# Reordering the sync engine's load queue in the cross-attention of a fused decoder layer

## What is computed

```python
q = (Q @ Wq.T).reshape(b, s, H, DK).transpose(0, 2, 1, 3)      # Q = norm(x), H = 16 heads of DK = 16
k = (K @ Wk.T).reshape(b, -1, H, DK).transpose(0, 2, 1, 3)     # K = V = ctx, 120 places a row
v = (V @ Wv.T).reshape(b, -1, H, DK).transpose(0, 2, 1, 3)
score = jnp.einsum('bhqd,bhkd->bhqk', q, k) / jnp.sqrt(jnp.float32(DK))
score = jnp.where(mask == 0, jnp.float32(1e-09), score)
out = jnp.einsum('bhqk,bhkd->bhqd', jax.nn.softmax(score, axis=-1), v)
return out.transpose(0, 2, 1, 3).reshape(b, s, d) @ Wo.T
```

## Time and profile before

| | us |
|---|---|
| median of 3 runs (1132.88 to 1135.84) | 1135.7 |
| the profiled execution | 1124.39 |
| its span, first to last instruction | 1122.6 |
| self-attention, to the barrier | 0 to 437 |
| cross-attention | 437 to 713 |
| experts | 713 to 1123 |

### The profile page before, as it was taken

The page is one execution under the profiler, slowest core; times in us unless marked ns, Lnnn a source line. Parts: engine busy times, 40 slices in busy tenths (PEclk is TensorE's granted clock), DMA queues, the critical chain, the costliest instruction groups (busy, mean ns, idle before and its releaser), DMA issues.

```text
span 1122.6 us, 28508 instructions
## 1 busy us (share of the span) xinstructions
PE 1061.1 (95%) x11049; PEld 913.5 (81%) x11049; DVE 668.2 (60%) x1317; ACT 646.5 (58%) x872; POOL 554.2 (49%) x678
## 2 busy tenths in 40 slices
PE   7799999999999988999998999999999999999995
PEld 6678777777777766777776777899999999999995
DVE  4488888888888878788886888423424222222221
ACT  2466666566666665777775777544454444444441
POOL 5534455453545233433654666567754444444442
PEclk9999999999999999999998999999999999999998
DMA  8674644637355432665665657675432323322322
GB/s 216 161 185 105 167 123 111 179 89 179 106 129 152 112 98 73 172 187 159 136 148 147 145 148 231 215 152 57 45 53 47 53 51 50 48 48 48 48 43 24
DMA packets 174562, 130.22 MB, mean 116 GB/s; under 512 B 60810, under 2 KB 162927, under 8 KB 174432
## 3 DMA queue, kind: packets, MB, share of 16 engines
q1 hardware_dynamic: 155280, 106.79, 36.6%
q0 software_dynamic: 15840, 18.77, 11.6%
q10 hardware_dynamic: 3312, 2.85, 0.9%
HBM read 88.29 MB, written 40.08 MB: 114 GB/s over the span
## 4 chain that ended last, share of the span: by engine, by line
PE 50%; DMA 5%; DVE 1%; ACT 1%; issue 1%; SPq 1%; POOL 0%; POOLq 0%; ACTq 0%
PE ps_scores L1987 22%; PE ps_out L2005 11%; PE ps_turn L1850 4%; PE ps_misc L1882 2%; DMA weights<-q_scr 2%; PE ps_out L1862 2%; PE ps_scores L1837 2%; PE ps_misc L1803 2%; DMA q_scr<-qp 1%; PE ps_turn L1966 1%; PE ps_misc L1870 1%; PE ps_scores L1830 1%; PE ps_misc L1876 1%; SPq L1499 1%; ACT weights L2178 1%
## 5 line engine op out<-in xcount | busy, mean ns | idle before, releaser
L1987 PEld LDWEIGHTS ps_scores<-xgT,weights 128*128 128x128 f32 x2272 | 264.1, 192 | 3.3
L1987 PE MATMUL ps_scores<-xgT,weights 128*128 128x128 f32 x2272 | 265.7, 275 | 0.0
L2476 DVE TENSOR_TENSOR gate<-ps_scores,silu 128x512 f32<-128x512 f32 x71 | 49.1, 692 | 241.3 <-ACT silu L2218 241.2
L956 ACT ACTIVATE weights<-ps_scores 128x1024 f32<-128x1024 f32 x128 | 127.1, 1023 | 78.2 <-PE ps_scores L631 63.7
L2218 ACT ACTIVATE silu<-ps_scores 128x512 f32<-128x512 f32 x71 | 42.4, 597 | 206.2 <-PE ps_scores L1987 206.1
L2005 PE MATMUL ps_out<-w2s,gate 128*128 x560 | 132.6, 380 | 0.8 <-DVE y L2482 0.8
L2211 ACT COPY weights<-weights 128x2048 f32 x68 | 129.9, 1911 | 0.0
L2005 PEld LDWEIGHTS ps_out<-w2s,gate 128*128 128x128 f32 x560 | 101.0, 190 | 11.9 <-issue 1.2
L1130 DVE TENSOR_REDUCE sa_rowmax<-ps_turn 128x8 bf16<-128x1024 f32 x64 | 77.8, 1216 | 34.4 <-PE ps_turn L608 34.3
L961 ACT CAST weights<-ps_scores 8x1024 bf16<-8x1024 f32 x64 | 64.3, 1004 | 54.1 <-PE ps_scores L622 54.1
L1673 POOL DMA_INDIRECT table<-entry,slot_i x64 | 64.9, 1014 | 43.6 <-PE ps_out L1862 19.9
(11 more groups left out here) (325 smaller groups left out, 2104.6 us busy)
## 6 DMA issues: line engine op xcount, KB each, us to landing
weights<-w_scr SPq DMA_DIRECT2D x60, 256.0 KB, 4.2
weights<-q_scr SPq DMA_DIRECT2D x96, 128.0 KB
ks<-w_scr SPq DMA_DIRECT2D x24, 256.0 KB, 3.8
weights<-k_scr SPq DMA_DIRECT2D x48, 120.0 KB, 3.8
w_scr<-wp SPq DMA_DIRECT2D x7, 768.0 KB, 3.9
q_scr<-qp SPq DMA_DIRECT2D x14, 384.0 KB, 3.6
weights<-in_w1T SPq DMA_DIRECT2D x10, 512.0 KB, 7.0
weights<-in_w3T SPq DMA_DIRECT2D x10, 512.0 KB, 9.6
```

The costliest lines, as they stand in the source:

```text
L956: act.activation(probs[s % 2][:], m.scores[s % 2][:], ACT.Exp, scale=SCALE).then_inc(exped, 1)
L1987: mm = pe.matmul(h_ps[r % 2][:, j, c, :], weights[:, j, k, c * P:(c + 1) * P], xgT[r % 2][:, k, :], start=(k == 0), stop=(k == DT - 1))
```

## The change

The self-attention block gets two more loads at its end, behind the queries of row 1: the keys of pair 1 (`stack_cross_keys(1)`, six DMAs) and the mask of row 2. The cross block no longer loads these at its start; it loads the values of three rows there, not of two.

In the loop the order of a row becomes: first half of the key stack (even rows from 2 on), `store_x`, `store_norm`, mask, `load_w2`, (tables), values, then `store_q` and both halves of the query stack of the same row b + 2 directly behind it, and last the second half of the key stack. Row 0 does only the mask, the query store and stack, and `load_w2`. The semaphore values of the waits follow the new places; the buffers and sizes are the same.

```diff
-        def stack_cross_keys():
-            sp.wait_ge(k_stored, 16 * R)
+        def stack_cross_keys(p):
+            sp.wait_ge(k_stored, 16 * R * (p + 1))
             sp.wait_ge(shifted, R * UPR * (NP - 1))
             for s, part in enumerate(K_PARTS):
-                if s > 2:
-                    sp.wait_ge(m.k_stacked[s % 3], 16)
+                if p + s // 3 > 0:
+                    sp.wait_ge(m.k_stacked[s % 3], 32 * p + 16 * (s // 3))
...
-        stack_cross_keys()
+        stack_cross_keys(0)
         stack_cross_queries(0)
         store_keys_values(NB - 1)
         stack_cross_queries(1)
+        stack_cross_keys(1)
+        sp.wait_ge(m.zero_done, 1)
+        sp.dma_start(m.mask[0], a["mask"][R].rearrange("(n p) k -> p n k", p=P)).then_inc(m.mask_in, 16)
...
-        load_v(0)
-        load_v(1)
-        load_mask(R)
+        for b in range(3):
+            load_v(b)
         sp.dma_start(routerT[:], a["routerT"].rearrange("(k p) e -> p k e", p=P)).then_inc(route_in, 16)
         expert_reg = sp.alloc_register("weights_of")
         for b in range(NB):
-            nxt_q, nxt_k = 0 < b < NB - 1, b < NB - 2 and b % R == 0
-            if nxt_q:
-                stack_q(b + 1, 0)
-            if nxt_q:
-                stack_q(b + 1, 1)
+            nxt_q, nxt_k = b < NB - 2, 0 < b < NB - 2 and b % R == 0
             if nxt_k:
                 stack_k(b // R + 1, 0)
             if b > 1:
                 store_x(b - 2)
                 store_norm(b - 2)
-            if nxt_k:
-                stack_k(b // R + 1, 1)
-
-            if b < NB - 2:
-                store_q(b + 2)
             if b < NB - 3:
                 load_mask(b + 3)
-            load_w2(b)
+            if b > 0:
+                load_w2(b)
             if b == 1:
                 load_routing()
             if b == 3:
                 store_blank()
-            if b < NB - 2:
+            if 0 < b < NB - 2:
                 load_v(b + 2)
+            if nxt_q:
+                store_q(b + 2)
+                stack_q(b + 2, 0)
+                stack_q(b + 2, 1)
+            if b == 0:
+                load_w2(b)
+            if nxt_k:
+                stack_k(b // R + 1, 1)
```

More of the change, by code:

```diff
@@ L335, in load_cross @@
                 sp.dma_start(m.mask[r], a["mask"][r].rearrange("(n p) k -> p n k", p=P)).then_inc(m.mask_in, 16)
-        def stack_cross_keys():
-            sp.wait_ge(k_stored, 16 * R)
+        def stack_cross_keys(p):
+            sp.wait_ge(k_stored, 16 * R * (p + 1))
             sp.wait_ge(shifted, R * UPR * (NP - 1))
             for s, part in enumerate(K_PARTS):
-                if s > 2:
-                    sp.wait_ge(m.k_stacked[s % 3], 16)
-                sp.dma_start(m.ks[0][s:KS:SLOTS].rearrange("k h r t -> k h (r t)"),
-                             m.k_scr[part, :, 0:R, :].rearrange("(h d) r t -> d h (r t)", d=HD))\
+                if p + s // 3 > 0:
+                    sp.wait_ge(m.k_stacked[s % 3], 32 * p + 16 * (s // 3))
+                sp.dma_start(m.ks[p][s:KS:SLOTS].rearrange("k h r t -> k h (r t)"),
+                             m.k_scr[part, :, R * p:R * p + R, :].rearrange("(h d) r t -> d h (r t)", d=HD))\
                     .then_inc(m.k_stacked[s % 3], 16)
@@ L388, in sync_program @@
         stack_cross_queries(1)
+        stack_cross_keys(1)
+        sp.wait_ge(m.zero_done, 1)
+        sp.dma_start(m.mask[0], a["mask"][R].rearrange("(n p) k -> p n k", p=P)).then_inc(m.mask_in, 16)
         for i in range(3):
-            sp.wait_ge(m.k_stacked[i], 32)
+            sp.wait_ge(m.k_stacked[i], 64)
             sp.wait_ge(m.q_stacked[i], 32 * R)
```

## The result

The changed kernel takes 1144.3 us (median of 10 runs, 1138.3 to 1153.5) beside 1135.8 us for the kernel before (10 runs, 1131.7 to 1143.0): a ratio of **1.0075, 95% interval 1.005 to 1.010**. It is slower by 8.5 us, where 9.0 us faster was forecast, and it lies outside the range of 1115 to 1136.

What follows compares the result with a forecast made beforehand. Cross-attention was taken as PE-bound except 62 us (540 to 602) waiting for late query stacks behind SP's landings. 10.96 us off, less 2 us for the second key half, gave 9.0 us: 1126.7 us, range 1115 to 1136.

Steps and rivals of the forecast that it cites:

- the second key half: Last load of an even row: lands at F + 24.9, just when needed; 0.5 us wait in four late pairs, 2 us.
- F: The prediction's time zero: the start of a row's queries on PE, 534.94 us in row 6.
- 10.96 us: Gain before the key half's cost: 9.36 for rows 6 to 10, plus waits of 0.72, 0.39 and 0.49 us.
- the queries' waits: PE's six waits for the query stack before a row's first scores, 8.52 us in sum; forecast to go.
- store to landing: Query store's landing in late rows: 4.7 us, at the upper end 6.0.
- stack issued: Issue of both halves of the query stack on SP's queue: 6.0 us, taken from 5.0 to 9.43.
- the term of 9.36: Excess of rows 6 to 10: 77.61 us against 68.25 without a wait; 6.92 are waits, most of the rest clock.
- the keys take the place of the queries: Rival, slower: late second key half delays even rows' first scores; 3.6 us in four late pairs for 0.3%; chance 0.07.
- work moved ahead of the store: Loads and stores issued before an even row's query store: some 5.1 us, done inside POOL's 6.64, costed at nothing.
- The timed runs wait more than the profiled one: Rival, faster: much of the timed runs' extra 11.3 us is these waits and goes too, up to 1115 us; chance 0.15.
- the border: Pair 1's keys and a mask before the barrier cost nothing, as SP waits 14.7 us there; row 2's 0.72 us goes.
- The rule of the Trainium skill: DMA engines take a queue's descriptors in ring order; against the change, as the store stands behind 1.5 MB, before 1.2.

Runs made afterwards that it cites:

- the second profile: The changed kernel run once more, unchanged, for another profile: 1.0067 of before; rows 6 to 13 took 131.7 us with 5.5 us of waits for keys.
- the scatters gone: Changed kernel with GpSimd's 32 scattering DMAs of rows 6 to 13 moved into row 14, one execution; ratio not read, rows 6 to 13 took 119.9 us.
- the second profile of before: The kernel before run again, unchanged: 0.9994 of before; rows 6 to 13 took 122.4 us with 2.6 us of waits for queries.
- the free halves: Kernel before, with a stack's second three loads no longer waiting for its first three to land, in the row loop: 0.9936 and 0.9969 of before.
- the last set: Runs on another chip of the kernel before, it with free halves (0.9969), and that with pair 1's keys and a mask loaded in the self-attention (0.9967).
- the changed kernel with rows 14 and 15 as before: Changed kernel with the query stacks of rows 14 and 15 put back one row after their store, first in their row: 1.0083 of before.
- the changed kernel with free halves: Changed kernel, with a stack's second three loads no longer waiting for its first three to land, queries and keys, in the row loop: 0.9972 of before.

## Why the prediction was wrong

The step that failed is the second key half. It was forecast to land at F + 24.9 and to cost 2 us in all; PE could start on it only at F + 26.5 to 30.6 in the rows below, and in the second profile three such waits cost 11.8 us. The gain set against it, 10.96 us, was too large as well.

**Right: the queries' waits go.** No profile of the changed kernel has a wait for the query load. The store goes out at F + 6.8 in rows 6 and 8 (second profile), and at F + 7.7 in row 8 of the first; forecast was F + 6.64.

**Wrong: the time of the second key half.** Two terms of the new chain were too small, and the last too large. Row 6 of the second profile stands above (queries at 536.5; its key half is issued at 558.59 in 1.91 us); in row 8 (queries at 575.63) SP's queue has:

```profile
582.46 0.37 SPq L1508 DMA_DIRECT2D q_scr<-qp  x1
589.27 7.27 SPq L1502 DMA_DIRECT2D weights<-q_scr  x6
596.58 1.91 SPq L1502 DMA_DIRECT2D weights<-k_scr  x3
```

| term, us | forecast | row 6 | row 8 | row 8, first profile |
|---|---|---|---|---|
| queries to store | 6.64 | 6.8 | 6.8 | 7.7 |
| store to landing | 4.7 | 7.8 | 6.8 | 8.5 |
| stack issued | 6.0 | 7.4 | 7.3 | 8.5 |
| key half issued | 2.1 | 2.0 | 2.0 | 2.0 |
| end of issue to PE's start | 5.5 | 2.9 | 3.6 | 3.9 |
| sum | 24.9 | 26.9 | 26.5 | 30.6 |

The store's landing was taken from rows in which little stood in front of it (4.7, at most 6.0), though the text names the 1.5 MB that would. The stack was put at 6.0, "near the stack with little ahead of it"; with the loads gone from ahead of it, it still took 7.3 to 8.5 us, and with the scatters gone too, 4.5 to 5.0. The errors cancel in part; what is left keeps PE waiting for 1.65 to 5.72 us, where 0.5 was allowed for.

**Wrong: the price of lateness.** "0.5 us of wait each" counts a wait once. The text had the other half in hand: in the term of 9.36 it found 2.44 us beyond the waits, most of it clock. With the clock the three waits of 5.5 us cost 11.8.

**Wrong: how much there was to win.** The 10.96 us came from one execution. In the second profile of before, rows 6 to 13 lose 2.6 us, not 9.7. By the timed runs all of the stacks' waits are worth 0.3 to 0.6%, or 3 to 7 us: that is what taking them away gives.

So of the four rivals, "the keys take the place of the queries" is what happened, and it had 0.07. It was held to need a landing at F + 28.3, 3.6 us late, in four pairs. Three pairs with 1.65 to 2.0 us were enough, because here the clock fell behind each and every us of wait cost about two, and because the gain against it was a quarter to two thirds of what was put there. (The rivals' chances also add up to 0.78 for "faster", not 0.76.)

**Wrong: work moved ahead of the store costs nothing.** The same move costs 12 to 13 us in before, and putting three of the loads between store and stack gives some 5 us back in the changed kernel. How much of the changed kernel's loss is these loads and how much the store's landing on SP's chain **stays open**, since no run took the loads from ahead of the store without putting them ahead of the stack or of the next store. Shown is the sum: without the waits inside a stack, all of it goes.

**The timed runs wait more than the profiled one**: not as that rival had it. With the free halves PE waits for no stack, and that is worth 3 to 7 us, not 9 and 11.3 more. Why the first profile of before is 11.3 us short is not shown; another chip would be enough for it, since chips differ by up to 12 us (before: 1120.5 to 1132.5 in the five sets, 1135.8 in the first).

**Right: the border is worth nothing, and the experts are not touched.** The 20 us behind row 13 look like a cost of the change in a comparison of two profiles, and are none. In the first profile of the changed kernel ACT stands idle twice, and DVE for 3.9 us at the longest, for something that no instruction or DMA of the profile released (line waited for, us in total, times, longest):

```profile
ACT silu L2220 <- remote: 12.4, 2, 7.2
```

The second profile has no such line, and the experts take 400.1 us, and the ratios of the timed runs of the two sets are nearly the same, 1.0075 and 1.0067. The kernel of before with free halves has it on the chip of the last set:

```profile
ACT silu L2216 <- remote: 16.5, 3, 6.8
```

All three kernels profiled on that chip, two of which have the loop order of before, show it, with 54 to 56 us from the queries of row 13 to the first expert and 402 to 406 us of experts; before took 1132.5 us there. None of the profiles of the other four sets has it, and there the experts take 400 to 401 us.

**The rule of the Trainium skill.** The store landed 7.8, 6.8 and 8.5 us after its issue where the row it was costed by says 4.7. "DMA: Bandwidth & Descriptors", section "Queues, rings and completion order", has each DMA engine take a queue's descriptors in ring order, which spoke against the change, and the runs agree with its sign: with the scatters gone the store lands in 6.8 us in row 4, directly behind the loads, and in 2.7 to 2.9 in rows 7 to 9, where 2.3 us and more lie between. How much of the 6.8 to 8.5 us of the late rows it makes is not shown, since the scatters run there too.

## What to carry to other kernels

Count the landings that an issuing queue waits for one behind the other in a period, with the durations of the stretch in question: a reorder that puts a store and its reload together adds a landing to that chain, and what stands last pays for it; take away waits in the queue that guard nothing before you reorder it. Price a wait of TensorE with the clock behind it: two waits of the same length cost 1.8 and 3.4 us here. Take a gain from more than one profile: a third or more of this one was not in the next, and neither was a "loss" of 20 us. And when you move work to the end of a loop's body, look at what it then stands ahead of in the next pass.

## What the hardware showed unexpectedly

- With four small scattering DMAs a row (0.5% of the DMA engines' time) a stack of six loads took 5.1 to 8.5 us to issue in rows 6 to 9 of the changed order, without them 4.5 to 5.0 us (one execution).
- A 384 KB store landed in 2.9 to 3.1 us where SP had issued nothing for over 3 us (rows 7, 9, 11 and 13 of before with free halves), and in 6.8 us directly behind 1.5 MB of loads and stores of its own queue, with no scatter near.
- A wait of TensorE of 1.64 us was followed by a granted clock of 1.00 and cost 1.8 us; one of 1.65 us by 0.92 over its row, and cost 3.4 us. What decides between the two was not found.
- SP can be held at an issue: three key loads take 1.9 us to issue in most rows, but 4.2 us in one of the changed kernel with rows 14 and 15 as before, and 4.8 us in the changed kernel with free halves, where they stand behind six loads that were issued in one go:

```profile
546.96 5.04 SPq L1500 DMA_DIRECT2D weights<-q_scr  x6
552.04 4.81 SPq L1500 DMA_DIRECT2D weights<-k_scr  x3
```

- On one chip ACT and DVE stood idle for 3.7 to 7 us at a time with nothing in the profile that released them, whatever the kernel. The first profile of the changed kernel has it too; on which chip that ran is not recorded. What it is was not found.
